# Q and K of the next head pair projected in 64-row tiles behind the scores of step 0, transposes of the last query tile one step later, V halved

## The reference

```python
q = (x @ Wq)            # 4 batches, 1024 tokens, 16 heads of 64, all float32
k, v = split(x @ Wkv)
s = einsum('bhid,bhjd->bhij', q * scale, k)
gm = max(s, axis=-1)    # over all columns, also the masked ones
p = where(causal_mask, 0.0, exp(s - gm))
out = einsum('bhij,bhjd->bhid', p, v) / (sum(p, -1) + EPS)
x = layernorm(x + out @ Wo + bo)
x = layernorm(x + ffn(x))   # token-shifted gate and squared relu, 128 wide
```

## Time and profile before

| | |
|---|---|
| median of 3 runs | 1263.97 us (1260.96 to 1264.96) |
| profiled execution, its own time | 1263.72 us |
| its span, first to last instruction | 1261.9 us |
| mean granted TensorE clock | 0.984 |
| busy share | TensorE 95%, VectorE 72%, ScalarE 61%, GpSimd 39% |

### The profile page before, as it was taken

The page is one execution under the profiler, slowest core; times in us unless marked ns, Lnnn a source line. Parts: engine busy times, 40 slices in busy tenths (PEclk is TensorE's granted clock), DMA queues, the critical chain, the costliest instruction groups (busy, mean ns, idle before and its releaser), DMA issues.

```text
span 1261.9 us, 22548 instructions
## 1 busy us (share of the span) xinstructions
PE 1192.6 (95%) x8051; PEld 794.7 (63%) x8051; DVE 911.8 (72%) x1780; ACT 770.9 (61%) x1730; POOL 490.8 (39%) x838
## 2 busy tenths in 40 slices
PE   6899999999999999999999999999999999999654
PEld 4666666666666666666666666666666666665343
DVE  5777777777777777777777777776777777777597
ACT  4666656666666566666666666666666666665254
POOL 4344444444444444444444444444444444442100
PEclk9999999999999999999999999999999999999887
DMA  4000000000000000000000000000000000000001
GB/s 140 18 2 18 17 18 18 18 18 18 2 18 18 18 18 19 18 18 1 18 18 18 18 18 18 18 2 18 17 19 18 18 18 18 2 18 18 17 18 50
DMA packets 25038, 24.98 MB, mean 20 GB/s; under 512 B 10464, under 2 KB 20448, under 8 KB 24928
## 3 DMA queue, kind: packets, MB, share of 16 engines
q1 hardware_dynamic: 24352, 23.14, 7.0%
q10 hardware_dynamic: 576, 0.39, 0.1%
HBM read 21.17 MB, written 2.36 MB: 19 GB/s over the span
## 4 chain that ended last, share of the span: by engine, by line
PE 78%; DVE 13%; issue 7%; DMA 1%; ACT 0%; POOLq 0%; POOL 0%; DVEq 0%; SPq 0%
PE ps_s L688 33%; PE ps_x L720 20%; PE ps_x L736 13%; DVE tile L509 8%; PE ps_x L625 6%; PE ps_x L747 4%; DVE stats L542 1%; PE ps_x L634 1%; DVE pt L564 1%; DVE tile L553 1%; DVE y L553 0%; DVE tile L608 0%; DMA pt<-in_L_attn_x 0%; DVE tile L605 0%; DMA rb<-recips 0%
## 5 line engine op out<-in xcount | busy, mean ns | idle before, releaser
L509 DVE TENSOR_SCALAR_CACHE_REDUCE tile<-ps_s 128x1024 f32<-128x1024 f32 x512 | 606.5, 1222 | 299.6 <-PE ps_s L688 297.2
L397 ACT ACTIVATE tile<-tile,neg_max 128x640 f32<-128x640 f32 (+7 forms) x512 | 396.4, 778 | 227.6 <-POOL tile L315 226.9
L688 PE MATMUL ps_s<-ks,qs 64*128 64x512 f32 x3072 | 427.0, 410 | 21.4 <-DVE tile L509 18.0
L315 POOL TENSOR_SCALAR_AFFINE_SELECT tile<-tile 128x128 f32<-128x128 f32 x512 | 149.7, 293 | 661.1 <-DVE tile L509 661.1
L688 PEld LDWEIGHTS ps_s<-ks,qs 64*128 64x128 f32 x3072 | 271.7, 185 | 134.2 <-DVE tile L509 77.0
L720 PEld LDWEIGHTS ps_x<-ident,tile 128*128 128x128 f32 x2304 | 259.1, 140 | 89.8 <-issue 68.0
L720 PE MATMUL ps_x<-ident,tile 128*128 128x128 f32 x2304 | 306.6, 276 | 0.1
L736 PE MATMUL ps_x<-pt,vs 128*64 128x512 f32 (+3 forms) x1536 | 269.9, 493 | 0.1
L410 ACT ACTIVATE pt<-ps_x 128x384 f32<-128x384 f32 (+3 forms) x384 | 165.8, 493 | 118.2 <-PE ps_x L720 118.2
L736 PEld LDWEIGHTS ps_x<-pt,vs 128*64 128x64 f32 x1536 | 102.2, 137 | 160.0 <-issue 150.8
L522 DVE COPY pt<-ps_x 128x384 f32<-128x384 f32 (+3 forms) x384 | 190.6, 546 | 2.6
(11 more groups left out here) (66 smaller groups left out, 443.3 us busy)
## 6 DMA issues: line engine op xcount, KB each, us to landing
rb<-recips SPq DMA_DIRECT2D x64, 256.0 KB, 3.9
out<-y SPq DMA_DIRECT2D x4, 512.0 KB, 3.2
y<-in_L_attn_x SPq DMA_DIRECT2D x3, 512.0 KB, 8.5
pt<-in_L_attn_Wkv SPq DMA_DIRECT2D x2, 384.0 KB, 6.8
pt<-in_L_attn_x SPq DMA_DIRECT2D x2, 256.0 KB, 4.4
wos<-in_L_attn_Wo SPq DMA_DIRECT2D x1, 512.0 KB, 7.1
recips<-recips_sb SPq DMA_DIRECT2D x32, 8.0 KB, 1.5
pt<-in_L_attn_Wq SPq DMA_DIRECT2D x1, 384.0 KB, 6.0
```

The lines of the kernel that those rows point to most:

```text
L315: pool.affine_select(out=block_of, in_=block_of, compare_op=ALU.is_ge, fill=fill, base=0, pattern=[[-1, P]], channel_multiplier=1).then_in ...
L397: act.activation(cols, cols, ACT.Exp, bias=neg_max[:, at:at + 1], scale=-1.0, accum_out=sums[:, p % 2, a, t:t + 1]).then_inc(s_exp, 1)
L509: dve.tensor_scalar(tile[:, at, :], ps_s[a][:, :], -SCALE, None, ALU.mult, ALU.min, accum_out=neg_max[:, at:at + 1]).then_inc(s_evac, 1)
L688: ins = mm(ps_s[a][:, c * HALF:(c + 1) * HALF], qs[rows, p % 2, qh, t * P:(t + 1) * P], ks[rows, p % 2, kh, c * HALF:(c + 1) * HALF], star ...
```

## The change

- The projections of all four quarters of the next pair now stand directly behind the scores of step 0 (`qk_of`). Each matmul of 128 rows becomes two of 64 rows. `project_both` does a group of two quarters at a time: in phase 0 the upper row half adds to the bank of one quarter and the lower row half to that of the other; in phase 1 the halves change places. The order is phase 0 of Q, phase 0 of K, phase 1 of Q, phase 1 of K; each phase 1 waits for the completion of its phase 0 (`s_phase`). That makes 24 matmuls in 12 pairs, in place of 12 matmuls in four steps.
- ScalarE copies all four quarters in step 0, ahead of the exponentials. `full` has four buffers; the two new ones lie in a part of `pt1` that the transposes don't use. GpSimd splits them in steps 0, 1, 3 and 5, as before.
- Tile 7 of the pair before is turned and copied in step 1, not in step 0.
- Of V's two halves one stays in step 1, the other goes to step 3. x moves from step 1 to step 5.

The diff, cut to its core:

```diff
-QK_AT = {0: 0, 1: 1, 3: 2, 5: 3}
-V_AT = 1
-X_AT = 1
+SPLIT_AT = {0: 0, 1: 1, 3: 2, 5: 3}
+V_AT = {1: 0, 3: 1}
+X_AT = 5
-TURN_AT = {0: ((1, 7),), 1: ((0, 0),), 3: ((0, 1), (0, 2)), 5: ((0, 3), (0, 4)), 7: ((0, 5), (0, 6))}
+TURN_AT = {1: ((1, 7), (0, 0)), 3: ((0, 1), (0, 2)), 5: ((0, 3), (0, 4)), 7: ((0, 5), (0, 6))}
...
-        full = [x1t[:, 1:1 + HALF], x1t[:, 1 + HALF:1 + N]]
+
+        full = [x1t[:, 1 + n * HALF:1 + (n + 1) * HALF].rearrange("p (j n) -> p j n", j=2) for n in range(2)]
+        full += [pt1[:, n, 6:8, 0:2 * P] for n in range(2)]
...
-                act.wait_ge(s_proj, done + 1)
-                at_least(act, s_qklo, done - 1)
-                act.activation(full[n % 2], ps_x[BANK["qk", p, 0, n]][:, :], ACT.Copy).then_inc(s_full, 1)
+
+                act.wait_ge(s_proj, done + 2 - n % 2)
+                at_least(act, s_qklo, done - 3)
+                act.activation(full[n], ps_x[BANK["qk", p, 0, n]][:, :].rearrange("p (j n) -> p j n", j=2), ACT.Copy
+                               ).then_inc(s_full, 1)
...
                     if t == 0 and p + 1 < ALL_PAIRS:
-                        take_qk(p + 1, 0)
+                        for n in range(4):
+                            take_qk(p + 1, n)
                     for q, u in turned_in(p, t):
                         take_turned(q, u)
-                    if t > 0 and t in QK_AT and p + 1 < ALL_PAIRS:
-                        take_qk(p + 1, QK_AT[t])
-                    if t == V_AT and p < ALL_PAIRS:
-                        take_v(p // 2, 2 * (p % 2))
-                        take_v(p // 2, 2 * (p % 2) + 1)
+                    if t in V_AT and p < ALL_PAIRS:
+                        take_v(p // 2, 2 * (p % 2) + V_AT[t])
...
+            def project_both(p, first, phase):
+
+
+                b, r = divmod(p, PAIRS)
+                what, _ = QK[first]
+                for m, (wh, xh) in enumerate(terms):
+                    for h in range(2):
+                        n = first + (h + phase) % 2
+                        c, rows = QK[n][1], slice(h * DH, (h + 1) * DH)
+                        ins = mm(ps_x[BANK["qk", p, 0, n]][:, :], ws[rows, "qk".index(what), wh, r * P:(r + 1) * P],
+                                 xs[rows, b % XSLOTS, xh, c * HALF:(c + 1) * HALF],
+                                 start=(phase == 0 and m == 0), stop=(phase == 1 and m == 2))
+                        if m == 2:
+                            ins.then_inc(s_proj if phase else s_phase, 1)
...
+            def qk_of(p):
                 b, r = divmod(p, PAIRS)
-                n = QK_AT[t]
-                unit = ("qk", p, 0, n)
-                if p == 2 and n == 0:
+                if p == 2:
                     pe.wait_ge(s_wlo, 3)
-                if r == 0 and n == 0:
+                if r == 0:
                     pe.wait_ge(s_xlo, 2 * b + 2)
-                drained(unit)
-                project_qk(p, *QK[n], ps_x[BANK[unit]], s_proj)
+                for first in (0, 2):
+                    drained(("qk", p, 0, first))
+                    drained(("qk", p, 0, first + 1))
+                    project_both(p, first, 0)
+                for first in (0, 2):
+
+                    pe.wait_ge(s_phase, 4 * (p - 1) + first + 2)
+                    project_both(p, first, 1)
...
-                    if t == 0:
-                        qk_of(p + 1, t)
+                    if t == 0 and p + 1 < ALL_PAIRS:
+                        qk_of(p + 1)
                     for q, u in turned_in(p, t):
                         turn_tile(q, u, 0)
-                    if t > 0:
-                        qk_of(p + 1, t)
-                    if t == V_AT and p < ALL_PAIRS:
-                        v_of(p, 0)
-                        v_of(p, 1)
+                    if t in V_AT and p < ALL_PAIRS:
+                        v_of(p, V_AT[t])
                     if t == X_AT and p < ALL_PAIRS:
```

More of the change, by code:

```diff
@@ L66 @@
     for _t in range(TILES):
-        _first = [("qk", _p + 1, 0, QK_AT[_t])] if _t in QK_AT and _p + 1 < ALL_PAIRS else []
         _quads = [[("quad", q, a, n) for q, u in turned_in(_p, _t) for n in range(FIRST_QUAD[u], FIRST_QUAD[u + 1])]
                   for a in range(2)]
[L70 to L75, removed]
+        if _t == 0 and _p + 1 < ALL_PAIRS:
+            UNITS += [("qk", _p + 1, 0, n) for n in range(4)]
+        UNITS += _quads[0]
+        if _t in V_AT and _p < ALL_PAIRS:
+            UNITS.append(("v", _p // 2, 0, 2 * (_p % 2) + V_AT[_t]))
         if _t == X_AT and _p < ALL_PAIRS:
@@ L182, in build @@
         s_lo0 = sem("s_lo0")
+        s_phase = sem("s_phase")
         s_proj = sem("s_proj")
@@ L301, in split @@
                 dst = qs if what == "q" else ks
-                hi, lo = (dst[:, p % 2, h, c * HALF:(c + 1) * HALF] for h in (0, 1))
+                hi, lo = (dst[:, p % 2, h, c * HALF:(c + 1) * HALF].rearrange("p (j n) -> p j n", j=2)
+                          for h in (0, 1))
                 done = 4 * (p - 1) + n
@@ L306, in split @@
                 pool.wait_ge(s_full, done + 1)
-                pool.tensor_copy(hi, full[n % 2]).then_inc(s_qkhi, 1)
+                pool.tensor_copy(hi, full[n]).then_inc(s_qkhi, 1)
                 pool.wait_ge(s_qkhi, done + 1)
-                pool.tensor_tensor(lo, full[n % 2], hi.bitcast(F32), ALU.subtract).then_inc(s_qklo, 1)
+                pool.tensor_tensor(lo, full[n], hi.bitcast(F32), ALU.subtract).then_inc(s_qklo, 1)
             def mask(p, t, a):
@@ L331, in _ @@
                         norm(p - 1, NORM_AT[t])
-                    if t in QK_AT and p + 1 < ALL_PAIRS:
-                        split(p + 1, QK_AT[t])
+                    if t in SPLIT_AT and p + 1 < ALL_PAIRS:
+                        split(p + 1, SPLIT_AT[t])
         @block.scalar
@@ L691, in scores @@
                                 ins.then_inc(s_scores, 1)
-            def qk_of(p, t):
-                if p >= ALL_PAIRS or t not in QK_AT:
-                    return
+            def qk_of(p):
                 b, r = divmod(p, PAIRS)
-                n = QK_AT[t]
-                unit = ("qk", p, 0, n)
-                if p == 2 and n == 0:
+                if p == 2:
                     pe.wait_ge(s_wlo, 3)
-                if r == 0 and n == 0:
+                if r == 0:
                     pe.wait_ge(s_xlo, 2 * b + 2)
-                drained(unit)
-                project_qk(p, *QK[n], ps_x[BANK[unit]], s_proj)
+                for first in (0, 2):
[5 more added lines that the diff above has]
+                    project_both(p, first, 1)
             def v_of(p, n):
```

## The result

| | before | changed |
|---|---|---|
| median of 18 runs each | 1262.62 us (1260.96 to 1264.96) | 1265.18 us (1263.54 to 1267.34) |
| ratio, 95% interval | | 1.002 (1.0013 to 1.0028) |
| span of the profiled execution | 1261.9 us | 1264.0 us |
| TensorE busy | 1192.6 us | 1183.8 us |

The account below looks back on a forecast made before the run. Bound: a loop of TensorE's scores and VectorE's evacuations. Ordinary pairs 0, x +1.1, last pair +1.2, first pair -0.3, small terms +0.3 gave +2.3 us, put at 1265.0 for overlap; 8-in-10 range 1258 to 1274.

Parts of the forecast that it names:

- The loop of VectorE and the scores: All steps: scores wait for VectorE to empty PSUM, a floor of about 4.22 us; only work beyond it costs time.
- step 5: Ordinary pairs: a projection goes, and the step falls from 4.39 to 4.21 us, 0.18 saved.
- Step 0: 12 projection pairs at 0.23 us replace 3 projections and 16 transposes; next scores 0.02 later, phase waits cost nothing.
- Step 1: Transposes come, projection and half of V go; TensorE ends the step, steps 0 and 1 together 0.18 us longer.
- The 0.11: Step 1's scores: extra delay behind their first pair, kept in the sum at 0.11 us, possible range 0 to 0.11.
- Step 3: Half of V (0.71 us) takes the place of a projection (0.70 us): no change.
- x: Moved to step 5 in six pairs: makes step 6 0.65 us late, net +0.18 each, +1.1 us in all.
- The last pair: Step 0 is left with idle time, the clock may fall in step 1: +1.2 us, from 0 to 1.8.
- The first pair: A projection leaves a step at the low clock: -0.3 us, with 1.3 either way.
- late banks on ScalarE's side: Rival, step 1: slower ScalarE copies make TensorE stand about 0.35 us per pair, 10.5 in all, 1275 us; chance 0.16.
- The phase waits: Rival, step 0: late completions at two waits make it 0.3 us longer, +9 in all, 1274 us; chance 0.05.
- VectorE didn't end step 1: Denies the rival that VectorE's limit ends steps 0 and 1, gaining 0.18 to 0.25 us a pair, 1258 us; chance 0.13.

Follow-up runs that it names:

- v_in_three: Changed kernel, but both halves of V are done in step 3 and none in step 1; 1281.75 us in one execution.
- phases_adjacent: Changed kernel, but each phase 1 follows directly behind its own phase 0, for Q and then for K; 1285.9 us in one execution.
- x_last: Changed kernel, but in step 5 the transposes of x and VectorE's subtraction come behind the last transposes and VectorE's copies; 1262.96 us in one execution.
- last_turn: Changed kernel, but in the last pair tile 7 of the pair before is turned in step 0, as before the change; 1262.49 us in one execution.
- both_ends: Changed kernel with tile 7 turned in step 0 in the last pair and x behind step 5's last transposes and copies; 1260.75 us, ratio 0.9982 to before.
- full_rows: Changed kernel, but the four projections behind the scores of step 0 are 12 matmuls of 128 rows, without phases; 1277.64 us in one execution.

## Why the prediction was right

The time (1265.0 for 1265.18) and the sign of the small change came out; "same" was the likeliest, and with 1.002 the change is within the 0.3%. That the time fits to 0.2 us is luck. I counted from 1263.97, the median of three runs; eighteen runs put it at 1262.62, 1.35 lower. And I made +1.0 of a sum of +2.3 because small terms overlap; measured is +2.6, and no run shows such an overlap. The two errors cancel. The sum itself, +2.3, fits the spans (+2.1), again with two large terms off in opposite directions, as said below. Point by point:

- **The loop of VectorE and the scores as the measure of each step.** Right. Shown by v_in_three (six matmuls of V worth 0.20 or 0.72 according to the step) and by step 5, where 0.17 for 0.18 was gained.
- **Step 0.** 523.43 - 519.22 = 4.21 for my 4.25: a projection pair takes 0.227 and not 0.230. The waits on `s_phase` cost nothing; phases_adjacent shows that they cost 0.36 each without the distance.
- **Step 1.** Steps 0 and 1 together were to grow by 0.20 by the chain, of which I took 0.18, and grew by 0.18 (8.63 for 8.45). Three terms were off and cancel. V's six matmuls took 0.80 for 0.71: behind transposes the first takes 0.20 to the next and not 0.12 (before, V stood behind projections, and the projections paid this). Nine transposes up to V took 0.96 for 1.03, and the projections 0.04 less in all. The 0.11 that I was unsure of is paid, because the scores wait for VectorE.
- **Step 3.** +0.03 for "nothing", for the same reason: V 0.80, the projection 0.78 with its own first matmul.
- **x.** Late by 0.62 for 0.65; shown by x_last.
- **The last pair.** Mechanism right, size too small: I took 1.2 of 0 to 1.8, it was 1.8 in step 1 and 0.2 more in its step 3, which now holds V.
- **The first pair.** -0.3 was taken, -1.96 measured, which is outside the 1.3 either way that I allowed. It isn't one number: four kernels that do the same work in pair 0 took 34.87 (the changed kernel), 34.81 (last_turn), 36.35 (x_last) and 34.66 (both_ends), according to where the low clock lay: in step 5 alone (5.27 and 5.26), in steps 3 and 5 (5.50 and 5.49), in step 3 alone (5.08). In the kernel before it lay in steps 3 and 5 too, and the pair took 36.83. Where it fell alike, then, 0.48 was gained (36.35 for 36.83), near my 0.3, and the other 1.5 goes with the execution, as far as one execution of each can tell. That the gain of the first pair made up for the loss of the last was luck.

The rivals: late banks on ScalarE's side didn't come, its four copies take 0.49, 0.48 and 0.48 to one another, and the margin at the first bank was 0.39 (526.78 - 526.31 less 0.08) against my 0.19. (I had priced that wait at 0.35; by its own times, 528.7 less 528.39, it would have been 0.3.) The phase waits didn't bite. VectorE didn't end step 1. The pairs run side by side.

The sum of the parts in the two profiles: 24 ordinary pairs +0.7, x +1.0, last pair +2.0, first pair -2.0, the part behind the scores +0.5, the part ahead of them -0.2, in all +2.1 with rounding. The part behind the scores isn't of the change's making: the instructions are the same, and the clock is what is seen to differ. The TensorE time that was spared went where it was worth little: step 5 gained 0.17 and now waits for 0.44, and step 1, full of work, gave the 0.2 back.

## What to carry to other kernels

Count each step by the loop that ends it: moved work is worth what it stood above that limit in the old place, less what it adds above it in the new one, and the busy time of the engine tells neither. A wait on an engine's own result is free when enough independent work of the same form stands between (three pairs of matmuls here), and costs a full restart when it doesn't (0.36 us each here). Look at the first and last round apart: where work has moved away from a round without a neighbour, the idle engine may pay with a slower clock, and filling the hole with work that nobody reads may be cheaper (here it came with 1.0 to 2.2 us less, the size not shown).

## What the runs showed of the hardware

- A pair of 64-row matmuls of 512 columns on both row halves takes 0.227 us in the projections of the changed kernel, one 128-row matmul 0.230 (mean of ten intervals in full_rows).
- In the places looked at, where TensorE started with its weights not loaded ahead the second matmul (or pair) came 0.33 to 0.34 behind the first in place of 0.23. A change of tile shape does this and adds 0.09 to 0.10 before; a wait alone does it too (0.34 in the changed kernel, 0.24 without a wait in phases_adjacent).
- Between transposes and other matmuls of the same tile shape the first of the new kind takes 0.08 more (V behind transposes 0.20 for 0.12, in step 1 of the changed kernel).
- TensorE idle for 2.56 us behind 1.65 of scores was followed by a mean clock of 0.72 in the last pair. In pair 0 the same gap of 2.47 ahead of step 3 was followed by scores at the low clock in x_last (2.93 for 12 matmuls) and at the full one in the changed kernel (1.65).
